# Macaron block, attention state products: one 128x128 matmul per chunk, or two 64x64 tiles read from the scan's result

## The reference

```python
q = (x @ W_q).reshape(Bn, Tn, H, dk)   # k and v alike
a = sigmoid(x @ W_gate + b_gate).reshape(Bn, Tn, H, dk)
def step(S, qkva):
    S = a_t[..., None] * S + k_t[..., None] * v_t[..., None, :]
    o_t = einsum('bhk,bhkv->bhv', q_t, S)
```

## Time and profile before

| | |
|---|---|
| Median of 3 runs | 2488.08 us (2481.18 to 2488.99) |
| The profiled execution | 2488.26 us |
| Its span, first to last instruction | 2486.5 us |
| PE busy over the span | 84% |
| DVE busy over the span | 58% |
| Attention's steps, about | 797 to 1672 us of the span |

### The profile page before, as it was taken

The page is one execution under the profiler, slowest core; times in us unless marked ns, Lnnn a source line. Parts: engine busy times, 40 slices in busy tenths (PEclk is TensorE's granted clock), DMA queues, the critical chain, the costliest instruction groups (busy, mean ns, idle before and its releaser), DMA issues.

```text
span 2486.5 us, 38276 instructions
## 1 busy us (share of the span) xinstructions
PE 2098.6 (84%) x13967; PEld 1808.2 (73%) x13968; DVE 1434.1 (58%) x3544; ACT 1188.6 (48%) x1927; POOL 265.1 (11%) x268
## 2 busy tenths in 40 slices
PE   5169999999995898989898898987099999999990
PEld 5058889898984676777767676767079898988890
DVE  6345554555445858677585958566245544555544
ACT  1055565665554544445454545431055555655540
POOL 1710000000003000101010000002700000000236
PEclk9999999999997999999999999985599999999995
DMA  6332221222211000000000000001422212222224
GB/s 248 129 107 95 93 77 53 78 80 85 94 55 41 12 9 10 16 3 18 1 18 5 14 1 1 1 1 38 145 76 90 76 53 78 72 93 93 66 64 136
DMA packets 95409, 150.89 MB, mean 61 GB/s; under 512 B 9583, under 2 KB 76678, under 8 KB 94068
## 3 DMA queue, kind: packets, MB, share of 16 engines
q1 hardware_dynamic: 83008, 116.46, 13.8%
q0 software_dynamic: 12288, 32.91, 4.2%
HBM read 98.84 MB, written 51.15 MB: 60 GB/s over the span
## 4 chain that ended last, share of the span: by engine, by line
PE 59%; DVE 17%; PEld 7%; POOL 6%; issue 6%; ACT 4%; DMA 1%; PEldq 1%; DVEq 0%; POOLq 0%; SPq 0%
PE bank L536 26%; PE bank L555 11%; PE bank L689 4%; POOL expert_in L424 4%; PEld bank L555 4%; PE bank L674 4%; PE bank L607 3%; PEld bank L536 3%; PE bank L677 3%; PE bank L631 3%; DVE wide L1287 2%; DVE wide L1276 2%; POOL halves L431 2%; DVE wide L1304 2%; DVE wide L1289 2%
## 5 line engine op out<-in xcount | busy, mean ns | idle before, releaser
L536 PE MATMUL bank<-halves 128*128 128x512 f32 (+2 forms) x3744 | 773.7, 367 | 22.3 <-DVE halves L1110 22.3
L536 PEld LDWEIGHTS bank<-halves 128*128 128x128 f32 x3744 | 651.2, 191 | 129.1 <-issue 24.6
L555 PE MATMUL bank<-halves 128*128 128x256 f32 (+1 forms) x3288 | 403.2, 283 | 3.0 <-issue 3.0
L555 PEld LDWEIGHTS bank<-halves 128*128 128x128 f32 (+1 forms) x3288 | 397.3, 189 | 5.6 <-issue 4.8
L791 ACT ACTIVATE temp<-bank,bias_now 128x512 f32<-128x512 f32 (+1 forms) x312 | 200.4, 642 | 371.0 <-PE bank L536 370.7
L1123 DVE SCALAR_TENSOR_TENSOR temp<-bank,bias_fc,temp 128x512 f32<-128x512 f32 (+1 forms) x312 | 216.0, 692 | 229.6 <-ACT temp L791 226.0
L607 PE MATMUL bank<-halves 128*128 128x512 f32 x1152 | 286.3, 400 | 2.0 <-DVE halves L1250 2.0
L1130 DVE TENSOR_TENSOR halves<-temp,halves 128x512 fp32r<-128x512 f32 (+1 forms) x312 | 198.0, 635 | 126.7 <-ACT halves L747 123.5
L607 PEld LDWEIGHTS bank<-halves 128*128 128x128 f32 x1152 | 212.2, 189 | 49.9 <-DVE halves L1250 2.4
L431 POOL DMA_INDIRECT halves<-expert_out,read_slot x96 | 103.7, 1080 | 1246.2 <-DMA expert_out<-rows 650.9
L1145 DVE TENSOR_TENSOR rows<-bank,rows 128x256 f32<-128x256 f32 (+1 forms) x160 | 66.8, 422 | 217.1 <-PE bank L555 191.0
(11 more groups left out here) (159 smaller groups left out, 2369.2 us busy)
## 6 DMA issues: line engine op xcount, KB each, us to landing
expert_out<-rows SPq DMA_DIRECT2D x144, 128.0 KB, 1.7
wide<-in_L_ffn_w_c_fc SPq DMA_DIRECT2D x16, 1024.0 KB, 5.3
wide<-in_L_ffn_w_gate SPq DMA_DIRECT2D x16, 1024.0 KB, 7.4
wide<-in_L_ffn_w_c_proj SPq DMA_DIRECT2D x16, 1024.0 KB, 5.4
wide<-expert_in SPq DMA_DIRECT2D x32, 512.0 KB, 4.8
expert_in<-halves SPq DMA_DIRECT2D x9, 1024.0 KB
x<-in_L_attn_x SPq DMA_DIRECT2D x4, 1024.0 KB, 9.9
out_x<-x SPq DMA_DIRECT2D x32, 128.0 KB, 2.3
```

Of the source, the lines that this page charges most:

```text
L536: m = pe.matmul(bank[at + b][:, 0:w], a[:, kc, j * P:(j + 1) * P], v[:, kc, 0:w], start=(i == 0), stop=(i == len(ps) - 1))
L555: mm = pe.matmul(bank[4 + t % 2][0:m, 0:C], a[:, j, o:o + m], v[:, j, :], start=(k == 0), stop=(k == len(ps) - 1))
```

## The change

`state_in` and its two copies go, and with them one memset ahead of the attention. The state products take their weights straight from `states`, at a distance of 24 bytes, and each is cut into two products of one head, 64 rows by 64 columns. All eight state products of a step now come first, then all eight products with the masked scores. Only the first chunk's state product of each head starts a new sum in the bank. Since PE now reads `states`, the next scan waits for a new semaphore `states_used`, and `state_ready` is given by the scan.

```diff
-ATT_CLEARS = 8
+ATT_CLEARS = 7
...
+                    by_chunk = states.rearrange("p (n c) -> p c n", n=DH)
                     for c in range(SUPER):
-                        cols = slice(c * P, (c + 1) * P)
-                        pe.matmul(bank[5][:, cols], state_in[:, c, :], qd[g % 2][:, c, :],
-                                  start=True, stop=False, skip_group_check=True)
                         for h in range(2):
-                            m = pe.matmul(bank[5][h * DH:(h + 1) * DH, cols],
+                            hp = slice(h * DH, (h + 1) * DH)
+                            m = pe.matmul(bank[5][hp, c * P:(c + 1) * P], by_chunk[hp, c + 1, :], qd[g % 2][hp, c, :],
+                                          start=(c == 0), stop=False, skip_group_check=True)
+                    m.then_inc(states_used, 1)
+                    for c in range(SUPER):
+                        for h in range(2):
+                            m = pe.matmul(bank[5][h * DH:(h + 1) * DH, c * P:(c + 1) * P],
                                           v_sb[:, c, g * P + h * DH:g * P + (h + 1) * DH], prob[h][:, c, :],
                                           start=False, stop=True, skip_group_check=True)
                     m.then_inc(o_done, 1)
...
-                v.memset(state_in, 0.0).then_inc(att_cleared, 1)
...
-                    steps.after(v.tensor_tensor_scan(states, bank[7][:, 0:DH * (SUPER + 2)], factors, 0.0,
-                                                     ALU.add, ALU.mult))
-                    for h in range(2):
-                        hp = slice(h * DH, (h + 1) * DH)
-                        ins = v.tensor_copy(state_in[hp, :, hp].rearrange("p c n -> p n c"), st[hp, :, 1:SUPER + 1])
-                    ins.then_inc(state_ready, 1)
+                    wait_past(dve, states_used, G)
+                    v.tensor_tensor_scan(states, bank[7][:, 0:DH * (SUPER + 2)], factors, 0.0,
+                                         ALU.add, ALU.mult).then_inc(state_ready, 1)
+                    dve.wait_ge(state_ready, G + 1)
                     v.tensor_copy(state[:, g, :], st[:, :, SUPER + 1]).then_inc(state_kept, 1)
```

More of the change, by code:

```diff
@@ L186, in macaron @@
         kdt = part(temp, 0, SUPER, P)
-        state_in = part(temp, 512, SUPER, P)
         state = part(temp, 1024, NPAIR, DH)
@@ L263, in macaron @@
         wo_done, wo_added = sem("wo_done"), sem("wo_added")
+        states_used = sem("states_used")
         stored = sem("stored")
```

## The result

The changed kernel takes **2409.5 us**, median of 4 runs (2407.5 to 2411.2), where the kernel before, on the same chip, takes 2488.5 (2481.2 to 2494.3): a ratio of 0.9687, 95% interval 0.967 to 0.9704, so 3.1% faster and 79 us less. The forecast was 2412, with a range from 2390 to 2437. The profiled execution after took 2407.5 us (span 2405.8) against 2488.3.

A forecast was written before the change was run, and what follows sets the result against it. A ring of DVE and PE, with DVE nearly full, was taken to bound the kernel. Seven supertiles at 8.7 us give 61, the last 15: 76 us off 2488.3 makes 2412, range 2390 to 2437.

The forecast's parts named there:

- DVE's copies: In each of 64 steps the two copies leave DVE's chain between scan and kept copy, saving 0.81 us.
- ACT next in line: ACT's logarithm is late next: the running sums' wait on DVE grows from 0.15 to about 0.45 us, 0.4 used.
- sixth to seventh: Step from the sixth pair's mask to the seventh's: 0.81 + 0.33 - 0.4 = 0.75 us saved.
- PE's `outputs`: PE's state and head products: two blocks of 16 matmuls at 0.65 us, 3.02 falling to 1.3, saving 1.7.
- A sign that the prediction had named for being wrong: The 16 state product loads on PE taking well over the additions' 0.60 us, or one head's after the other's.
- the bound that the text gave: In PE's `outputs`, 1.16 us for both blocks of 16 matmuls would save 0.7 us.
- The eighth pair: PE's `outputs` are waited for on both sides, by state and output projection: 0.81 + 1.7 = 2.5 us saved.
- The last supertile: No next supertile to prepare: five steps save 2.05 us each, the seventh 2.5, the end 2.5; together 15.
- ACT not waited for: Rival: running sums find ACT's logarithm ready, 0.4 us falls away in 40 steps: 2396; chance 0.72 together with the forecast.
- Slow loads: Rival: strided weight loads make the state products' block 1.76 us and `outputs` 2.4, saving 56 in all: 2432; chance 0.12.
- One at a time: Rival: two heads' products in one bank take turns, block 3.5 us, `outputs` 4.2; 26 us slower, 2514; chance 0.03.
- The clock: Rival: PE waits more, granted clock falls, 1.75 us each; here and there 0.07 (to 2440), most steps 0.03 (about 2500).

The follow-up runs named there:

- sums_later: The changed kernel with DVE's running sums for the third to sixth pairs moved behind the next supertile's gathering and statistics; 2392.4 us, ratio 0.9617.
- half_columns: The changed kernel with state and head products moving only the first 64 of 128 columns, half of each output left out; 2409.2 us in one run.
- contiguous: The changed kernel plus one DVE copy behind the scan that sets the states side by side, so the tiles' weights have no stride; 2415.1 us, ratio 0.97.
- reorder_only: The kernel before with its four 128x128 state products ahead of the eight head products, copies and `state_in` kept; 2441.4 us, ratio 0.9812.
- contiguous_half: The changed kernel with weights copied side by side and only 64 of 128 columns moved, half of each output left out; 4078 us in its one execution.

## Why the prediction was right, point by point

**The total** was right within 3 us, 2412 for 2409.5, but one of its terms was mis-sized, and others made up for it, which is in part luck.

**DVE's copies**, 0.81 us a step: right. Scan to kept copy now follow at 1015.55 and 1016.54 without anything between, and the new wait for `states_used` does not show.

**ACT next in line**, a wait of 0.15 that becomes 0.45: right, 0.46 in the step above. Steps two to five of the middle supertile save 0.87, 0.93, 0.59 and 1.80 where 0.8, 0.8, 0.55 and 1.75 were worked out, and the first saves nothing, as said. sums_later confirms the cause: taking ACT's lateness off DVE's path gave a good half of the waiting back. One step was sized too low: sixth to seventh saves 1.11, not 0.75, in the main since ACT is waited for there for only 0.17 us and not 0.4.

**PE's `outputs`: the step that failed.** The prediction put the two blocks of 16 matmuls at 0.65 us each, because "the load sets the pace", and so a saving of 3.02 - 1.3 = 1.7 us. Measured: 2.03 us, a saving of 0.99. The row that was taken, the 16 of the `additions` in 0.60 us, moves 64 columns; the new products move 128, like the scores, and these stood beside it with 1.16. The head products of half_columns show that 128 moving columns set the pace where the load is contiguous, and contiguous shows the same for the state products: loads of 134 ns, and still 1.09. A sign that the prediction had named for being wrong was there too: the 16 loads of the state products took 1.01 us (the step after, above), well over the 0.60 of the additions. The price could have been had from the row of before: 3.02 us less seven changes of 0.17 leaves 1.83 of work, and one change makes it 2.0. So the bound that the text gave, a saving of 0.7 with 1.16 for both blocks, was nearer than the value taken.

It shows where PE is waited for on both sides. The eighth pair saves 1.81 us (38.39 to 36.58), which is 0.81 + 0.99, not 2.5:

```profile
1072.34 1.17 PE L677 MATMUL bank<-wide 64*64 64x128 f32 x16 [0.34 <-issue]
1073.44 1.09 PE L682 MATMUL bank<-wide 128*64 128x128 f32 x16
1075.95 2.29 PE L694 MATMUL bank<-halves 128*128 128x256 f32 x17 [1.42 <-DVE halves L1317]
```

Seven of these, at 0.7, are 4.8 us too much. Elsewhere the smaller saving was enough to take nearly all of DVE's waits at the mask away, so it cost little there, and with the step that was sized too low a supertile saves 8.56 us where 8.7 were forecast.

**The last supertile**: 15 forecast, of which 12.75 ahead of its last mask, where 11.0 were measured; its end would be 1.8 rather than 2.5 if it goes as the eighth pair does in the others. All but the first of its steps are 8.57 to 8.92 us, not 8.43. Without the next supertile's work DVE reaches the running sums earlier still, and waits longer for ACT than the 0.4 that was used for all steps:

```profile
1537.21 1.57 DVE L1262 TENSOR_TENSOR_SCAN wide<-wide,limit 128x64 f32<-128x64 f32 x8 [0.59 <-ACT wide L871]
1538.83 0.68 DVE L1291 TENSOR_TENSOR wide<-bank,causal 64x512 f32<-64x512 f32 x1
...
1546.25 1.57 DVE L1262 TENSOR_TENSOR_SCAN wide<-wide,limit 128x64 f32<-128x64 f32 x8 [0.97 <-ACT wide L871]
```

**What made up for it**: the 3.0 us of two clock falls that went, and 7.4 us ahead of the first mask and behind the last, of which the 1.8 above is a part and the rest is open; the runs of before themselves differ by 13 us. Neither was in the sum, so it was luck that they covered what the sum had too much.

**The rivals.** *ACT not waited for*: fell, since the waiting for ACT inside the steps grew from 13 to 35 us. *Slow loads*: its premise held in part, since two strided loads hold a pair for 0.113 us where contiguous ones let it go after 0.058 (the rival had taken 0.22), but 128 moving columns hide them; its 2.4 us for `outputs` was nearer to the truth than the forecast's 1.3, for another reason. *One at a time*: fell. The two heads' tiles start some 35 ns apart in the records, and a pair takes 0.109 us with contiguous weights, no longer than one pass of the full 128x128 product in the records of reorder_only (0.111), although both are row tiles that write the same bank. The scores, row tiles that write a bank each, take 0.112 a pair, so sharing the bank costs nothing here. The Trainium skill's rule in "TensorEngine Tiling (Array Packing)", section "Restrictions and Gotchas", that different row tiles cannot access the same bank at the same time, is not borne out here, where the two write different partitions of it. *The clock*: no falls in this kernel, but half_columns shows that the danger was real and of the size that was given.

## What to carry to other kernels

Price a matmul by the longer of its moving columns and its load, and take the price from a row that has the same number of moving columns, and not the same weights alone. Count the places where one kind of product follows the other: grouping four and four was worth 45 of 79 us here and needs neither a new tile nor a copy less. When time is taken from an engine that is nearly full, ask what it waits for next, and put work that is ready ahead of that wait: moving one call of the running sums gave another 16 us.

## What the hardware showed that was not expected

A strided load of 64 float32 weight columns, at 24 bytes' distance, takes 193 ns in the mean against 134 contiguous, and two of them hold a pair of products at 0.113 us; almost nothing of it is seen while 128 columns move. A pair of 64x64 tiles on different rows and columns of the array, writing one bank, takes as long as one full pass (0.109 and 0.111 us), so cutting a block-diagonal product into tiles saved no time on PE here; what it saved is the copy that builds the matrix. And one execution of contiguous_half ran with PE at half its pace throughout, while its granted clock reads 1.00. The group of the mixture's first products, which takes 366 ns a matmul in the kernel after:

```profile
L537 PE MATMUL bank<-halves 128*128 128x512 f32 (+2 forms) x3744 | 1538.6, 607 | 24.9 <-DVE halves L1115 22.7
```

Its single matmuls mostly start 0.44 us apart, where those of the kernel after start 0.22 apart. That is about the pace that the lower level of the clock (1.2 GHz) would give: in the kernel after, in a stretch with a granted clock of 0.50, the few matmuls of this group start 0.42 apart. The trace of this execution holds no record of the clock at all, where each of the others holds between 16 and 42, so its 1.00 is no measurement. That the clock was low throughout is likely and not shown, and why it should have been stays open; it did not come again.
